# Carrying the last probability column to its rows with small DMAs instead of with GpSimd, a matmul and VectorE

## The reference

```python
x = x + xattn(layernorm(x), ctx)      # 8 heads of 64; softmax over 257 context rows
x = x + attn(layernorm(x))            # a recurrence over the 32 positions with learned decay
x = x + ffn(layernorm(x))             # rank 64, 1024 hidden, gelu
# xattn:
attn = softmax(einsum('bhsd,bhld->bhsl', q, k) * 64 ** -0.5, axis=-1)
out  = einsum('bhsl,bhld->bhsd', attn, v)
```

## Time and profile before

| | |
|---|---|
| median of three runs | 970.15 us (969.84 to 971.87) |
| the profiled execution, its own time | 969.11 us |
| its span in the profile | 967.1 us, 2.0 us less than its time |
| PE busy | 943.9 us, 98% of the span |
| ACT, DVE busy | 607.3 us and 613.0 us, 63% each |
| POOL busy | 373.8 us, 39% |
| TensorE's granted clock | 1.00 of full speed throughout |
| DMA engines | 82 GB/s mean |

### The profile page before, as it was taken

How to read it: one execution, slowest core, us unless ns; L and a number is a source line. 1 busy time by engine, 2 the same in 40 slices (tenths; PEclk the granted TensorE clock), 3 DMA queues, 4 the chain that set the end, 5 groups by cost and what they waited for, 6 DMA issues and landing times.

```text
span 967.1 us, 23520 instructions
## 1 busy us (share of the span) xinstructions
PE 943.9 (98%) x9012; PEld 783.6 (81%) x9012; DVE 613.0 (63%) x1286; ACT 607.3 (63%) x1487; POOL 373.8 (39%) x484
## 2 busy tenths in 40 slices
PE   9999999999999999999999999999999999999998
PEld 7767888787888878798887878888787888877775
DVE  4765858476685847668485666747567584746461
ACT  3545657667575766767576675757757566674533
POOL 1423534244352524435253352524326252433330
PEclk9999999999999999999999999999999999999999
DMA  8314231322323132132222313122222313222000
GB/s 304 120 51 124 59 105 49 100 81 65 105 78 90 51 101 81 60 110 61 88 69 87 95 60 94 60 87 89 81 80 81 90 49 89 87 73 72 9 12 22
DMA packets 58013, 79.03 MB, mean 82 GB/s; under 512 B 10288, under 2 KB 39856, under 8 KB 57904
## 3 DMA queue, kind: packets, MB, share of 16 engines
q1 hardware_dynamic: 56192, 76.38, 25.9%
q10 hardware_dynamic: 1712, 1.16, 0.4%
HBM read 73.05 MB, written 4.46 MB: 80 GB/s over the span
## 4 chain that ended last, share of the span: by engine, by line
PE 78%; DVE 9%; ACT 7%; issue 3%; POOL 1%; DMA 0%; DVEq 0%; POOLq 0%; ACTq 0%
PE gb L369 16%; PE scores L428 7%; PE acc L459 7%; PE gb L492 6%; PE acc L455 6%; PE scores L432 6%; PE ptp L442 5%; PE acc L460 5%; PE gb L613 3%; PE gb L602 3%; DVE xn L840 3%; ACT probs L685 3%; PE gb L401 3%; DVE probs L853 2%; DVE small L846 2%
## 5 line engine op out<-in xcount | busy, mean ns | idle before, releaser
L1100 POOL TENSOR_TENSOR t_l<-raw_t,t_h 128x516 fp32r<-128x516 f32 x128 | 167.5, 1309 | 193.6 <-PE scores L432 131.0
L685 ACT ACTIVATE probs<-scores,small 128x257 f32<-128x257 f32 x256 | 119.1, 471 | 134.6 <-DVE small L846 134.4
L846 DVE TENSOR_REDUCE small<-scores 128x2 f32<-128x514 f32 x128 | 88.3, 690 | 127.5 <-PE scores L432 127.4
L1109 POOL TENSOR_TENSOR ptm<-probs,head 128x32 f32<-128x32 f32 x128 | 35.1, 274 | 261.9 <-DVE probs L853 261.9
L853 DVE TENSOR_TENSOR probs<-probs,small 128x514 f32<-128x514 f32 x128 | 101.7, 794 | 4.4
L459 PE MATMUL acc<-pt,raw_n 128*128 128x256 f32 x256 | 89.6, 431 | 0.0
L442 PE MATMUL ptp<-ident,probs 128*128 128x128 f32 x512 | 78.7, 276 | 10.5 <-DVE probs L853 9.4
L696 ACT ACTIVATE pt<-ptp 128x512 f32<-128x512 f32 x128 | 77.2, 603 | 13.2 <-PE ptp L442 11.7
L455 PE MATMUL acc<-pt,raw_n 128*64 128x128 f32 x1024 | 82.7, 282 | 2.3 <-ACT pt L696 0.4
L428 PE MATMUL scores<-t_h,qk_h 128*128 128x258 f32 x256 | 83.3, 325 | 0.0
L455 PEld LDWEIGHTS acc<-pt,raw_n 128*64 128x64 f32 x1024 | 55.4, 136 | 31.9 <-issue 21.0
(11 more groups left out here) (178 smaller groups left out, 2768.8 us busy)
## 6 DMA issues: line engine op xcount, KB each, us to landing
raw_t<-in_ctx_t SPq DMA_DIRECT2D x128, 258.0 KB, 3.3
raw_n<-in_ctx_n SPq DMA_DIRECT2D x128, 192.0 KB, 2.4
xb<-in_x SPq DMA_DIRECT2D x16, 256.0 KB, 4.3
vsp<-tail_values SPq DMA_DIRECT2D x256, 2.0 KB
out<-ob SPq DMA_DIRECT2D x16, 256.0 KB, 2.9
xin<-in_x SPq DMA_DIRECT2D x15, 256.0 KB, 2.9
khat<-in_wq ACTq DMA_DIRECT2D x1, 512.0 KB, 4.3
wv<-in_wv SPq DMA_DIRECT2D x1, 512.0 KB, 6.3
```

The source lines that it names most:

```text
L685: go(probs[n % 2][:, r, 0:L], scores[:, r, 0:L], ACT.Exp, bias=nmax[:, r:r + 1], accum_out=rsum[:, r:r + 1]).then_inc(s["exp_ready"], 1)
L846: v_.tensor_reduce(nmax[:], scores[:, :, 0:L], AX.X, ALU.max, negate=True)\
L1100: p_.tensor_tensor(t_l[m % 2][:], raw_t[m % RING][:], t_h[m % 2][:].bitcast(F32), ALU.subtract)\
```

## The change

The last column now goes straight from `probs` to `psp` with two DMAs per batch on the SP queue, one for each `r`. Each takes one element from each of 128 partitions and writes them as 4 rows of 32. `psp` has two buffers, zeroed once at the start; the DMAs write the places that are not zero, the same in every group. `exps` waits for these DMAs (`tail_in`) instead of for GpSimd, and `WV` waits for the 16 DMAs of its group. The piece `TP`, VectorE's `psp`, GpSimd's product, and the tables `head`, `same` and `diag` with their loads are gone. GpSimd still waits for `probs_ready` at the same place. `vsp` now gets only the half that is used: 8 DMAs per group instead of 16. The matmuls that warm TensorE up read zeros instead of ones.

```diff
-         ["TP"]]
+         []]
...
+        tail_in = [sem(f"tail_in{i}") for i in range(2)]
...
                 for h in range(H):
                     cols = slice(h * DH, (h + 1) * DH)
-                    for half in range(2):
-                        sp.dma_start(vsp[half * 64 + h:half * 64 + 64:H, cols], scratch[g * G:(g + 1) * G, cols])\
-                            .then_inc(vsp_in, 16)
+                    half = h // 4
+                    sp.dma_start(vsp[half * 64 + h:half * 64 + 64:H, cols], scratch[g * G:(g + 1) * G, cols])\
+                        .then_inc(vsp_in, 16)
+
+            def tail_column(n):
+                g, b = n // G, n % G
+                if n == 0:
+                    sp.wait_ge(s["psp_ready"], 1)
+                sp.wait_ge(s["probs_ready"], n + 1)
+                if b == 0 and g > 1:
+                    bank, k = BANK["WV1", g - 2]
+                    sp.wait_ge(bank_filled[bank], k)
+                for r in range(2):
+                    row = 64 * r + H * b + 4 * r
+                    sp.dma_start(psp[g % 2][row:row + 4, b], probs[n % 2][:, r, L - 1:L]).then_inc(tail_in[n % 2], 16)
...
                     n = i * G + b
+                    if n < B:
+                        tail_column(n)
                     if n + RING + 1 < B:
                         load_t(n + RING + 1)
...
-            def turn_tails(g):
-                out_ = tile("TP", g)
-                pe.wait_ge(s["ptm_ready"], (g + 1) * G)
...
-                drained("TP", g)
-                pe.wait_ge(vsp_in, 256 * (g + 1))
+                for t_in in tail_in:
+                    pe.wait_ge(t_in, 16 * G * (g + 1))
+                pe.wait_ge(vsp_in, 128 * (g + 1))
...
                 if n > 1:
-                    act.wait_ge(s["ptm_ready"], n - 1)
+                    act.wait_ge(tail_in[n % 2], 32 * (n // 2))
...
-            GAPS = [[["psp-1"], ["S2-2", "S3-2"], ["WV0-1", "WV1-1"]],
+            GAPS = [[[], ["S2-2", "S3-2"], ["WV0-1", "WV1-1"]],
...
-            v_.memset(ones, 1.0).then_inc(s["ones_ready"], 1)
+            v_.memset(zeros, 0.0)
+            v_.memset(psp[0][:], 0.0).then_inc(s["psp_ready"], 1)
...
                     if 0 <= n + 1 < B:
-                        tail_column(n + 1)
+                        pool.wait_ge(s["probs_ready"], n + 2)
```

More of the change, by code:

```diff
@@ L166, in build @@
         mask = sb("mask", [P, P], U8)
-        head = sb("head", [P, 2, 2, H])
-        same = sb("same", [P, G])
-        diag = sb("diag", [P, S])
         raw_t = [sb(f"raw_t{i}", [P, 2, LP]) for i in range(RING)]
@@ L181, in build @@
         pc = sb("pc", [P, H + H // 2, T])
-        ptm = [sb(f"ptm{i}", [P, 2, 2, G, H]) for i in range(2)]
-        psp = sb("psp", [P, G, S])
-        ones = psp[:].rearrange("p b s -> p (b s)")
+        psp = [sb(f"psp{i}", [P, G, S]) for i in range(2)]
+        zeros = psp[1][:].rearrange("p b s -> p (b s)")
         vsp = sb("vsp", [P, INNER])
@@ L263, in build @@
         scratch = nc.dram_tensor("tail_values", [B, INNER], F32, kind="Internal").ap()
-        SMALL = [(mask_raw, a["mask"]), (bw_raw, a["bw"]), (head[:], a["head"]), (same[:], a["same"]),
-                 (diag[:], a["diag"]), (vecs[:, 0:2], a["ln_g"]), (vecs[:, 2:4], a["ln_b"]),
+        SMALL = [(mask_raw, a["mask"]), (bw_raw, a["bw"]),
+                 (vecs[:, 0:2], a["ln_g"]), (vecs[:, 2:4], a["ln_b"]),
                  (vecs[:, 6:14], a["b1"])]
@@ L477, in wz_product @@
                 done("WZ", 0, last)
-            def turn_tails(g):
-                out_ = tile("TP", g)
-                pe.wait_ge(s["ptm_ready"], (g + 1) * G)
-                for r in range(2):
-                    last = mm(out_[:, 0, 0:S], ptm[g % 2][:, r].rearrange("p a b h -> p (a b h)"), diag[:],
-                              start=r == 0, stop=r == 1)
-                done("TP", g, last)
             def wv(g):
@@ L501, in wv @@
                         rows_ = slice(64 * (h // 4), 64 * (h // 4) + 64)
-                        head(h, vsp[rows_, h * DH:(h + 1) * DH], psp[rows_].rearrange("p b s -> p (b s)"), start=i == 1)
+                        head(h, vsp[rows_, h * DH:(h + 1) * DH], psp[g % 2][rows_].rearrange("p b s -> p (b s)"), start=i == 1)
                     for h in pairs[i]:
@@ L641, in stay_busy @@
                 for k in range(count):
-                    mm(ptp[:, 0], ones[:, 0:P], ones, start=True, stop=True)
-            pe.wait_ge(s["ones_ready"], 1)
+                    mm(ptp[:, 0], zeros[:, 0:P], zeros, start=True, stop=True)
+            pe.wait_ge(s["psp_ready"], 1)
             stay_busy(WARM)
@@ L922, in step @@
                     drain(n, g, v_.tensor_tensor(wz_l[:], t[:], wz_h[:].bitcast(F32), ALU.subtract))
-                elif n == "psp":
-                    t = wait_tile("TP", g)
-                    drain("TP", g, v_.tensor_tensor(
-                        psp[:], t[:, 0:1, 0:S].to_broadcast([P, G, S]),
-                        same[:].rearrange("p (b o) -> p b o", o=1).to_broadcast([P, G, S]), ALU.mult))
                 elif n == "Y1":
@@ L1005, in _ @@
                     [[], ["S0-1", "S1-1"], ["xn0+2"]]]
-            AT_END = [[[["psp-1"], ["S2-2", "S3-2"], ["WV0-1", "WV1-1"]],
+            AT_END = [[[[], ["S2-2", "S3-2"], ["WV0-1", "WV1-1"]],
                        [[], [], ["Y1-1"]],
@@ L1257 @@
         "x": np.ascontiguousarray(np.asarray(x).reshape(B * S, D)), "ctx_t": ctx_t, "ctx_n": ctx_n,
-        "ctx_tail": ctx_tail, "head": np.ascontiguousarray(head), "same": same, "diag": diag,
+        "ctx_tail": ctx_tail,
         "wq": chunks(np.asarray(L0_xattn_Wq)), "wk": wk, "wv": wv, "wo": chunks(np.asarray(L0_xattn_Wo)),
```

23 lines of the change are left out of this document (5 added, 18 removed).

## The result

The changed kernel took **963.74 us**, the median of four runs (963.18 to 964.78); beside them the kernel before took 970.76 us (969.84 to 971.87). The ratio is 0.9928, with a 95% interval of 0.9911 to 0.9946: 7.0 us less, where 4 were forecast. A second series gave 963.81 us and 0.9929 (0.9916 to 0.9941).

A forecast was written before the change was run, and what follows sets the result against it. TensorE's own list, busy 98% of the span, was taken as the bound nearly everywhere. Terms: -4.75 (TP) + 0.8 (tail's landing in group 0) = -3.95 us, from the median 970.15 to 966.2 us; range 964.2 to 971.2 us.

The forecast's parts named there:

- both are off PE's path: nothing: Dropping POOL's 35.1 us of products and DVE's 16 builds of psp was claimed to change the time by nothing.
- nothing either: At the start, one more memset and three loads fewer lie under the first load of x: no effect.
- rival D: Without POOL's product DVE's chain work speeds up, giving back one eighth of 35.1 us, 4.4 us: 962 us, chance 0.09.
- Its order stays: POOL loses its products but keeps its wait for the normalization at the same place, so its order is unchanged.
- TP: Piece removed from TensorE's list: 0.36 or 0.37 us at each of 13 group borders, 13 x 0.365 = 4.75 us less.
- Rival C: PE comes 0.36 us earlier but stands as much longer at a later wait of the group: 970.9 us, chance 0.15.
- Its sign: Mark of no gain in the profile after: PE's waits in total grow by 4 us or more.
- The landing: Second tail DMA, from its own issue: 1.8 us fixed + 32 x 0.024 = 2.6 us; slow end 6.3 from first issue.
- The wait in group 0: ScalarE's exponential behind the vsp burst starts 0.8 us late, arriving in full at PE; ends 0 and 3.9 us.
- the price of a packet: Small rows on the DMA queue taken at 0.024 us each, 32 for each of 4 engines in a tail DMA.
- SP: Two tail DMAs per step at 0.585 us issue each, hidden; after the burst raw_t goes out some 3.5 us earlier.
- Rival B: Tail DMAs land late in every group, delaying ScalarE's exponential behind the vsp burst: slower, 977.5 us, chance 0.10.

The follow-up runs named there:

- before_same_last: The kernel before with the 32-byte table `same` allocated last, so tiles behind it start 32 bytes lower (64 modulo 128): 967.12 us, ratio 0.9958.
- after_shift32: The kernel after with an unused 32-byte tile allocated ahead of all that the removed tables stood ahead of: 967.34 us, ratio 0.9968.
- after_pool_product: The kernel after with GpSimd's 128 x 32 product put back in each step, on constants, output unused: 960.36 us, ratio 0.9902.
- vsp_spread: The kernel after with the 8 vsp DMAs of a group spread over the steps with b = 4 to 7: 962.72 us, ratio 0.992.
- before_shift32: The kernel before with an unused 32-byte tile behind `same`, so tiles begin at 0 modulo 128: 970.96 us, ratio 1.0005.
- product_b5: The kernel after with GpSimd's product on constants put back only in the steps with b = 5: 963.58 us, ratio 0.9923.
- after_no_pool_wait: The kernel after without GpSimd's wait for the probabilities in each step: 991.48 us, ratio 1.021.
- after_16_vsp: The kernel after with 16 vsp DMAs per group again, half of them into rows that nothing reads: 1001.43 us, ratio 1.0313.

## Why the prediction was wrong, and where it was right

**The step that failed** is "both are off PE's path: nothing", with "nothing either" for the memset and the loads. In a sum that went by instructions, the removal of three tables and of a product on an idle engine had no term. The runs put two there. "Over 13 groups" below is the sum over the groups themselves, groups 2 to 14, in the traces:

- *Placement of the tiles.* Missing. It is worth 3.9 us (`before_same_last`, same instructions) or 2.9 us (`after_shift32`, from the other side); 3.6 and 2.6 us over 13 groups.
- *GpSimd's product.* The prediction had zero, and rival D a gain. Taking it out is a loss of 3.2 us at equal clock, 2.7 us over 13 groups (`after_pool_product`). "Its order stays" was true; its timing didn't. With nothing to do behind its wait, GpSimd starts its next operations 0.2 us sooner, and they fall on other operations of VectorE's chain. Rival D looked at the product beside VectorE and not at what comes after it: what the product made longer, the normalization of b = 7 by 0.9 us, it made up for and more on the two operations ahead of it.

The measured 963.7 us is nearer to rival D's 962 than to the forecast, but that is no merit of D: its mechanism has the opposite sign.

**TP**, 4.75 us: right in place and size, 0.364 us a border in the trace against 0.365, and 5.0 us when put back. Rival C, that PE stands as long at a later wait, is refuted by that: two matmuls nobody waits for cost their full time. Its sign, PE's waits growing by 4 us or more, was a bad one. It stood at 3.8 and 4.1 us in the two profiles of the kernel after, and 2.0 us come with the placement alone (`before_same_last`), where PE waits longer because its other work is done sooner.

**The landing**: 2.1 us against 2.6, both from the second DMA's issue. The wait in group 0 costs 0.4 us, taken away by `vsp_spread`, against 0.8. The fixed part was right and the price of a packet was not. In the 0.5 us of the trace in which the first of the two moved its data there are 132 packets (a view of the DMA queues; the busy share is 14.6% of 16 engines; the first line is that share in 40 slices, in tenths):

```profile
DMA  0000000000001233334343433342100000000000
DMA packets 132, 0.00 MB, mean 1 GB/s; under 512 B 132, under 2 KB 132, under 8 KB 132
...
q1 hardware_dynamic: 132, 0.00, 14.6%
```

That is 0.146 x 16 x 0.5 / 132 = 0.009 us a packet, where I had taken 0.024; with 32 of them in a row 0.3 us, and 1.8 us would be fixed. By the slices nearly all of it took some 17 x 0.0125 = 0.2 us. The 132 are 128 elements and four more, as if four engines each reported their end. By the page "DMA: Bandwidth & Descriptors" in the Trainium skill (why a DMA increments its semaphore by 16) it is four engines. The count agrees with it; the slices don't settle it, since a share of four tenths of 16 is six packets at once, and no row names the engines.

**SP**: 0.61 us a tail DMA (0.585 taken), `raw_t` 3.35 us earlier behind the burst (3.5). **Rival B** didn't occur, but for the 0.4 us in group 0.

**The sum as it should have been.** Over 13 groups the change itself is -6.5 us in the traces. TP is -4.9 there, the product +2.7, and the placement -3.6 as `before_same_last` has it: together -5.8, so 0.7 us are missing. With the placement as `after_shift32` has it (-2.6) the sum is -4.8, and 1.7 us are missing; the three effects were measured from different kernels and needn't add up. (The medians of the ledger give -0.40 - 0.27 + 0.20 = -0.47 us a group against -0.47 measured; that they close so well is luck of the medians.) One half of the 0.7 can be placed: the step with b = 2 of group 10 is 0.35 us longer than that step usually is in the three kernels with the old program, and in none with the new one. Why was not looked at. Groups 0 and 1 add 0.67, of which 0.4 is the tail. The starts of group 0 differ by 0.6 us between executions of like kernels, and the profiled execution of before is 0.7 us shorter than the mean of its clock, so single spans can't be closed better than that. The measured -6.5 us of whole executions at equal clock has 0.3 us outside the span (time less span is 2.06 us before and 1.79 after, means at clock 1.000).

From the forecast of -3.95 us to these -6.5: placement -3.6 and product +2.7, both missing; TP 0.15 more and groups 0 and 1 0.13 less; and 1.4 us without an experiment behind them. The kernel with the tiles placed as before, `after_shift32`, took 966.3 us at clock 1.000, next to the forecast of 966.2. That is luck: in it the missing loss by the product is made up for by what stays unexplained.

**Open.** Why the placement matters. Three remainders modulo 128 were tried (96, 64, 0; in bytes modulo 256 they are 224, 192 and 0), and all tiles moved together: neither the modulus nor which pair of tiles decides is shown. The lower clock appeared in the same step in the profiles of after, `before_shift32`, `before_same_last`, `product_b5` and `after_no_pool_wait`, in others not; why PE's idle time is followed by it only sometimes is not shown. For the other executions there is the mean clock alone, and that their 0.998 is this same step was not looked at. That GpSimd's later start is what shortens VectorE's chain at b = 6 and 7 is read from the traces; it was not tried with a bare delay in place of a product. The two best ingredients, the placement at 64 modulo 128 and the product, are both in `after_pool_product`; other placements than three were not tried.

## What to carry to other kernels

A change that adds or removes a small tile moves every tile behind it. Before a difference of a few tenths of a per cent is put down to the instructions, compare a kernel in which only the placement differs, and once a kernel is tuned try two or three placements: here 32 bytes were worth 0.3 to 0.4%. An idle engine isn't free to be made idler or freer: when its waits keep it away from another engine's operations, both what it waits for and how long it works then are part of the schedule. Look at single rows for this; a mean over all batches hid one normalization in eight that took 1.6 us instead of 0.7. And where a new transfer stands in a queue, what counts is what stands ahead of it: the tail DMAs cost 0.4 us behind 8 small DMAs and 38 us behind 16, a part of it through the clock, which fell where PE was made to wait.

## What the runs showed of the hardware

- Rounded matmuls with 256 columns followed each other at 113.8 to 119.8 ns according to where their tiles began in SBUF; `k` and `r` differed most (113.8 against 119.8 ns).
- With GpSimd's wait taken out, `xn` took 1.11 us instead of 0.61 and the normalization 0.88 instead of 0.70 on average, and the kernel was 28 us slower. VectorE's operations with a tensor in the matmul's output memory kept their length (`qk_l`, 0.68 us).
- The same normalization took 0.69 or 1.6 us, by what GpSimd did beside it.
- A DMA of 128 elements of 4 bytes between two places of SBUF made 128 packets and four more, moved them in some 0.2 us, and landed 2.1 us after its issue; the issue took 0.61 us of the queue.
- PE's 1.87 us of idle time in the last group were followed by the clock's lower level for some 3.4 us in one execution, at a cost of 1.36 us, and 1.86 us at the same place by none in another. With 6.25 and 3.79 us of idle time (`after_16_vsp`) the clock fell both times.
